# A Mamba block with quantised gate: softplus in phases, dt_proj's steps in a row, low-rank preparation by items, SiLU as one function

## Chip, cores and metric

One Trainium2 chip, one core. The time is device microseconds of one execution; all arrays are float32, the quantised weights int32.

## What is computed

x has the shape 2 x 1024 x 512 (batch, tokens, H). Cut to what matters:

```python
xn = layernorm(x)
p = xn @ in_proj_w                    # 512 -> x part 1024, z part 1024
xc = silu(conv4(x_part) + conv_b)     # causal, 4 taps, per channel
ssm = xc @ x_proj_w.T                 # 1024 -> 64: dt_r 32, B 16, C 16, each rmsnorm'd
dt = softplus(dt_r @ dt_proj_w.T + dt_bias)
h_t = exp(dt * A) * h_{t-1} + dt * B_t * xc_t     # 16 states a channel
y = (sum_n h * C + D * xc) * silu(z)
s = y @ out_proj_w.T
# qlinear: w = (q - 7.5) * scale * 0.005 ; x @ w.T + 0.02 * (x @ A @ B)
g = silu(qlinear_down(silu(qlinear_gate(xn)) * qlinear_up(xn)))
out = x + s * g
```

## The kernel before, in words

The program orders every engine's instructions by hand, with semaphores between them. It treats one batch b after the other, and within a batch two halves h of 512 channels (DH = 4 blocks of 128). TensorE is PE, VectorE DVE, ScalarE ACT, GpSimd POOL; SP issues most transfers, ACT's queue the stores of prepared weights.

**In_proj stage.** In eight rounds (m = 0 to 7) TensorE computes the x part of block m + 1 into one of two buffers of psA (`x_part`, L785, matmuls L748). ScalarE starts the convolution with bias and last tap (`start_conv`, L583), VectorE adds three taps (`conv`, L1032), ScalarE takes Tanh (L594), and VectorE makes silu from it (`conv_silu`, L1042; the taps were halved, L1022). TensorE's `x_proj(m-1)` (L790) follows x_part(m+1): per block eight matmuls with xc as the stationary operand and 64 columns to stream.

**Preparation, batch 0 only.** The FFN's weights become float weights with the low-rank product added. `ffn_weights(it)` (L992) on VectorE dequantises tile it (0 to 10: a gate and an up tile of 126 columns; 11 to 21: a tile of down) and adds the product that `low_rank(use)` (L752, matmuls L759 and L763, contraction over 32 rows) put into one of three PSUM banks. PT = 3 tiles go into each round, so the gate/up tiles are done in the first four rounds and down in the rest. Gate/up tiles go out to w_gu in device memory over ACT's queue (L602), with a wait for the additions, and come back in the scan stage. SP loads q tiles in a ring of three (`load_q`, L379).

**From x_proj to dt_proj.** ScalarE squares and copies the sums (L606, L607), VectorE reduces and scales them (L1057 to L1071), and TensorE turns them (L829); two quarters of the first `gate_up` (L766) stand before that. ScalarE copies the turned sums (L613).

**Softplus phase**, once per half. `dt_proj(i)` (L834) for the four channel blocks, and with it softplus as relu(v) + log(1 + exp(-|v|)) with a correction for what 1 + e loses in rounding: ScalarE makes |v| and relu (`relu_abs`, L617), exp and 1 + e (`one_plus_exp`, L628), Ln (`log`, L636). VectorE makes the correction (`lost`, L1074), takes it from the logarithm and adds relu (`softplus`, L1081: two steps). The blocks follow one another, with two temporaries for two blocks in turn. GpSimd multiplies dt by xc for blocks 0 to 2 (L522) and VectorE for block 3 (L1170). Beside this TensorE computes gate and up tiles (`ahead`), and in h=1 turns the sums of the half before back (`turn_back`, L848) for `finish_y` (L1090, two VectorE steps). A phase ends with four scans of state 0.

**Scan stage.** 16 states times four blocks a half: GpSimd makes dt·x·B (L529), ScalarE exp(dt·A) (L646), VectorE scans (L1104), TensorE transposes (L871). Beside it run gate/up, z and down. Then out_proj (L948) and the output.

Softplus after the phases' start, on ScalarE (L691 to L701):

```python
for i in range(DH):
    if i == 0 and h == 0: ahead(0)
    relu_abs(i)
    if i == 3: ahead(2 - h)
    if i: log(i - 1)
    one_plus_exp(i)
    if i == 1: ahead(1 - h)
```

## Time and profile before

| | |
|---|---|
| median of 3 runs | 1370.32 us (1368.41 to 1370.78) |
| the profiled execution's own time | 1369.48 us |
| its span, first to last instruction | 1367.7 us |
| mean granted TensorE clock | 0.938 |
| busy: PE, DVE, POOL, ACT | 88%, 75%, 56%, 54% of the span |

How to read it. Times are us from the start of the span. A timeline row gives start, length, engine, line, operation, output and inputs with their shapes, how many records are merged, and in brackets the idle time before and what ended it; the ends of matmuls are modelled and pass the next start by some 0.1 us, so a stretch is best taken from start to start. A float32 matmul leaves two records. A row by form gives the count, the busy time in all, the mean in ns of one, and the idle time before. A row of busy time by stretch gives the stretch and its length, then the busy us (and records) of PE, PEld (weight loads), DVE, ACT and POOL, the granted clock (1.00 is 2.4 GHz, 0.50 is 1.2), and the share and GB/s of the DMA engines.

### The profile page before, as it was taken

The page shows a single profiled execution, that of the slowest core. Times are in us where ns is not written, and L with a number is a line of the kernel's source. Part 1 is how long each engine was busy: PE and PEld are TensorE (multiplying, and loading weights), DVE is VectorE, ACT ScalarE, POOL GpSimd, SP SyncE. Part 2 cuts the span into 40 slices and gives each one's busy share as a digit, 9 for nine tenths or more (in the row PEclk, how much of TensorE's full clock was granted, in tenths as well). Part 3 has the DMA queues.
Part 4 walks back from the last instruction along what each step waited for, and adds up shares of the span by engine and source line. Part 5 has one row for each costly group of instructions (what it writes and reads, how often), then busy time and mean ns, then how long its engine had stood idle before and what let it go on. Part 6 is the DMA issues. An engine that isn't in the chain of part 4 may idle for free.

```text
span 1367.7 us, 13293 instructions
## 1 busy us (share of the span) xinstructions
PE 1208.3 (88%) x4598; PEld 662.3 (48%) x4598; DVE 1030.8 (75%) x827; ACT 735.3 (54%) x892; POOL 762.6 (56%) x418
## 2 busy tenths in 40 slices
PE   4999838999987799998999982999998779999898
PEld 3664415555543355555544541555554335555543
DVE  2866479999948999996415547999984899999631
ACT  3111577777728577773012266777762857777300
POOL 1000048999913799994130004899881379989411
PEclk9778879999999899999999977999999889999999
DMA  6542114999961199998701111499996119999841
GB/s 216 197 152 76 54 46 115 229 221 229 228 153 62 62 216 228 225 220 223 275 32 39 46 39 50 124 229 217 230 217 154 62 62 225 226 224 218 226 179 38
DMA packets 60612, 214.08 MB, mean 157 GB/s; under 512 B 6362, under 2 KB 6490, under 8 KB 60132
## 3 DMA queue, kind: packets, MB, share of 16 engines
q0 software_dynamic: 16128, 88.09, 33.5%
q1 hardware_dynamic: 42836, 119.50, 25.4%
q10 hardware_dynamic: 1584, 5.68, 1.0%
q8 instruction: 36, 0.59, 0.2%
q14 instruction: 28, 0.23, 0.1%
HBM read 102.18 MB, written 22.98 MB: 92 GB/s over the span
## 4 chain that ended last, share of the span: by engine, by line
PE 39%; POOL 32%; DVE 11%; issue 7%; DMA 6%; ACT 6%; POOLq 0%; SPq 0%; DVEq 0%; ACTq 0%
POOL ub L529 27%; PE psA L748 9%; PE psM L893 8%; PE psM L948 8%; POOL yT L540 4%; DVE hb L1104 4%; PE psT L871 4%; DMA yT<-yc 4%; PE psM L774 3%; PE psM L795 2%; DMA bn<-ss_rows_scratch 2%; DVE hb L973 1%; PE psT L759 1%; DVE ub L973 1%; DVE hb L1086 1%
## 5 line engine op out<-in xcount | busy, mean ns | idle before, releaser
L529 POOL TENSOR_TENSOR ub<-dtx,bn 128x1024 f32<-128x1024 f32 x256 | 646.3, 2580 | 72.8 <-DVE hb L1104 53.8
L1104 DVE TENSOR_TENSOR_SCAN hb<-psA,ub 128x1024 f32<-128x1024 f32 x256 | 579.8, 2281 | 24.4 <-POOL ub L529 13.3
L646 ACT ACTIVATE psA<-dt,cc 128x1024 f32<-128x1024 f32 x256 | 286.4, 1119 | 171.8 <-DVE hb L1104 171.1
L871 PE MATMUL psT<-ident,hb 128*128 128x128 f32 x2048 | 289.9, 280 | 92.3 <-DVE hb L1104 52.2
L774 PE MATMUL psM<-xnT,w_ts 128*126 128x512 f32 x704 | 343.9, 620 | 30.0 <-DVE hid L973 22.1
L871 PEld LDWEIGHTS psT<-ident,hb 128*128 128x128 f32 x2048 | 235.8, 142 | 261.7 <-issue 81.8
L665 ACT ACTIVATE yc<-psT,ssm 128x512 f32<-128x512 f32 x336 | 217.3, 678 | 45.9 <-PE psT L871 45.8
L522 POOL TENSOR_TENSOR dtx<-dt,xc 128x1024 f32<-128x1024 f32 x12 | 28.2, 2352 | 364.2 <-DVE dt L1088 364.2
L774 PEld LDWEIGHTS psM<-xnT,w_ts 128*126 128x126 f32 x704 | 128.0, 199 | 148.0 <-issue 122.4
L893 PE MATMUL psM<-w_dn,hid 126*128 126x512 f32 x352 | 170.3, 613 | 0.0
L973 DVE SCALAR_TENSOR_TENSOR yT<-psT,ssm,yT 128x512 f32<-128x512 f32 x144 | 105.4, 736 | 45.5 <-DMA yT<-yc 40.9
L748 PE MATMUL psA<-xnT,w_ts 128*128 128x512 f32 x256 | 125.9, 650 | 1.4 <-ACT xnT L574 1.4
L883 PE MATMUL psM<-xnT,w_ts 128*128 128x512 f32 x256 | 119.1, 593 | 0.0
L540 POOL DMA_DIRECT2D yT<-yc x112 | 110.0, 982 | 14.0 <-ACT yc L665 14.0
L948 PE MATMUL psM<-dt,xc 128*128 128x512 f32 x256 | 111.7, 592 | 0.0
L558 POOL TENSOR_TENSOR hid<-hid,dtx 128x512 f32<-128x512 f32 x16 | 20.1, 1263 | 130.3 <-DMA hid<-x_dram 76.8
L973 DVE SCALAR_TENSOR_TENSOR hb<-psA,cc,hb 128x1023 f32<-128x1023 f32 (+2 forms) x48 | 61.5, 1281 | 41.2 <-ACT hb L586 40.1
L893 PEld LDWEIGHTS psM<-w_dn,hid 126*128 126x128 f32 x352 | 63.9, 198 | 53.6 <-issue 53.6
L748 PEld LDWEIGHTS psA<-xnT,w_ts 128*128 128x128 f32 x256 | 52.6, 211 | 64.7 <-issue 62.6
L973 DVE SCALAR_TENSOR_TENSOR th<-th,psM 128x512 f32<-128x512 f32 (+1 forms) x92 | 61.4, 668 | 28.2 <-ACT th L687 17.6
L948 PEld LDWEIGHTS psM<-dt,xc 128*128 128x128 f32 x256 | 47.8, 190 | 56.0 <-issue 55.0
L687 ACT ACTIVATE th<-psM 128x512 f32<-128x512 f32 x48 | 28.1, 584 | 83.4 <-PE psM L893 76.4
(88 smaller groups left out, 785.8 us busy)
## 6 DMA issues: line engine op xcount, KB each, us to landing
yT<-yc POOLq DMA_DIRECT2D x112, 768.0 KB, 7.1
bn<-ss_rows_scratch SPq DMA_DIRECT2D x64, 512.0 KB, 6.1
w_ts<-w_gu_scratch SPq DMA_DIRECT2D x44, 504.0 KB, 4.5
w_ts<-w_in_dram SPq DMA_DIRECT2D x32, 256.0 KB, 4.4
z_scratch<-th SPq DMA_DIRECT2D x32, 256.0 KB, 4.5
hb<-z_scratch SPq DMA_DIRECT2D x16, 512.0 KB, 8.3
w_gu_scratch<-hid ACTq DMA_DIRECT2D x11, 504.0 KB, 3.1
yT<-x_dram SPq DMA_DIRECT2D x2, 2048.0 KB, 12.3
```

Of the source, the lines that this page charges most:

```text
L529: pool.tensor_tensor(ub[:, i % 2, :], dtx[:, i, :], bn[:, t, :], ALU.mult).then_inc(s_u, 1)
L540: pool.dma_start(yT[:, YD + e * YG:YD + e * YG + YG, :].rearrange("p a c -> p (a c)"), yc[:, ring(n, e), :, :].rearrange("p a c -> p (a c) ...
L646: act.activation(psA[:, i % 2, :], dt[:, i, :], ACT.Exp, scale=negA[:, h * DH + i, bass.ds(n, 1)]).then_inc(s_a, 1)
L665: act.activation(to, psT[:, Y_POS[tb] % 2, :], ACT.Copy, scale=ssm[:, tb, R + NS + n:R + NS + n + 1]).then_inc(s_tcp, 1)
L748: mm = pe.matmul(psA[:, dst, c * 512:(c + 1) * 512], w_is[:, t, k, :], xnT[:, k, c * 512:(c + 1) * 512], start=(k == 0), stop=(k == HK - 1))
L774: mm = pe.matmul(psM[0:IM, gu, :], w_ts[:, t, at:at + IM], xnT[:, k, h * CH:(h + 1) * CH], start=(k == 0), stop=(k == HK - 1))
L871: mm = pe.transpose(psT[:, at % 2, i * P:(i + 1) * P], hb[:, t * DH + i, tb * P:(tb + 1) * P], ident[:, :])
L883: mm = pe.matmul(psM[:, c, :], w_is[:, off % 2, k, :], xnT[:, k, c * 512:(c + 1) * 512], start=(k == 0), stop=(k == HK - 1))
L893: mm = pe.matmul(psM[:, j % 2, :], hid[0:IM, k, j * P:(j + 1) * P], w_dn[0:IM, k, :], start=(k == 0), stop=(k == IT - 1))
L948: mm = pe.matmul(psM[:, tb % 2, :], xc[:, k, tb * P:(tb + 1) * P], w_o[:, k, :], start=(k == 0), stop=(k == DB - 1))
L973: return dve.scalar_tensor_tensor(out=out, in0=in0, scalar=scalar, in1=in1, op0=op0, op1=op1)
L1104: dve.tensor_tensor_scan(hb[:, t * DH + i, :], psA[:, i % 2, :], ub[:, i % 2, :], 0.0, ALU.mult, ALU.add).then_inc(s_scan, 1)
```

## The change

- **Preparation by items.** `low_rank(j)` computes for item j the gate and the up product in turn, from one stacked pair of operands (gate in rows 0 to 31, up in 32 to 63, down in 64 to 95), and then down's. `dequantise(j)` and `add_low_rank(j)` do the same on VectorE. The eleven items lie evenly in the eight rounds (`prepared(m)`): two at m = 2, 5 and 7, otherwise one. Loads of q and stores of w_gu follow that order.
- **SiLU as one function.** ScalarE's Silu writes xc; the halving of the taps and VectorE's product go.
- **x_proj** has the weights as the stationary operand (64 columns) and streams xc, 512 columns a matmul, with the two halves of the tokens in the output partitions 0 to 63 and 64 to 127. The sums are then copied (xr) and turned by four transposes before the Square.
- **Softplus in phases.** ScalarE does four times Abs and Relu, then four times exp and 1 + e, then four Ln, then the decays. Temporaries are dtx[i] and ub or hb, one pair for each block. VectorE's `lost` also takes the correction from relu, in front of the logarithm, so that `softplus` is one step. dt·xc is VectorE's for all blocks (`drive`).
- **dt_proj** 0 to 3 stand in a row in h=0; in h=1 turn_back(0) and (1) stand before dt_proj(2) and (3). Gate/up comes behind them; only one quarter of it stays before the turning of the sums.

The diff, cut:

```diff
+def prepared(m):
+
+    return range(IT * m // DB, IT * (m + 1) // DB)
...
-            return (hb[:, DH, :], hb[:, DH + 3, :]) if i % 2 else (ub[:, 0, :], ub[:, 1, :])
+            return dtx[:, i, :], [ub[:, 0, :], ub[:, 1, :], hb[:, DH, :], hb[:, DH + 3, :]][i]
...
-                    for i in range(DH - 1):
-                        k = blk(b, h, i)
-                        pool.wait_ge(s_dt, k + 1)
-                        pool.tensor_tensor(dtx[:, i, :], dt[:, i, :], xc[:, h * DH + i, :],
-                                           ALU.mult).then_inc(s_dtxp, 1)
-                    pool.wait_ge(s_dtxp, (b * HALVES + h + 1) * (DH - 1))
...
                     act.wait_ge(s_af, a_use(b, m) + 3)
-                    act.activation(tmp[:, 2 + m % 2, :], tmp[:, m % 2, :], ACT.Tanh).then_inc(s_thc, 1)
-                    for j in range(PT):
-                        if m + 1 < DB and j == PT - 1:
-                            start_conv(m + 1)
-                        it = PT * m + j
-                        if b == 0 and it < IT:
-
-                            act.wait_ge(s_lrr, 2 * it + 5)
-                            act.dma_start(w_gu[it], wf[:, it % QD, :]).then_inc(s_wst[it % QD], 16)
-
-                v = psM[:, 0, :].rearrange("p (a e) -> p a e", e=E)
+                    act.activation(xc[:, m, :], tmp[:, m % 2, :], ACT.Silu).then_inc(s_xc, 1)
+                    if m + 1 < DB:
+                        start_conv(m + 1)
+                    if b == 0:
+                        for j in prepared(m):
+
+                            act.wait_ge(s_lrr, 3 * j + 5)
+                            act.dma_start(w_gu[j], wf[:, j % QD, :]).then_inc(s_wst[j % QD], 16)
+
                 act.wait_ge(s_xp, b + 1)
+                act.activation(xr, psM[:, 0, :], ACT.Copy).then_inc(s_xr, 1)
+                v = psT[:, 0, :].rearrange("p (a c e) -> p c a e", c=2, e=E)
+                act.wait_ge(s_xt, b + 1)
                 act.activation(sq, v, ACT.Square).then_inc(s_sq, 1)
-                act.activation(ssm[:, :, :], v, ACT.Copy).then_inc(s_xpr, 1)
+                act.activation(ssm[:, :, :].rearrange("p (c a) e -> p c a e", c=2), v, ACT.Copy).then_inc(s_xpr, 1)
...
-                        if i >= 2:
-                            act.wait_ge(s_dt, k - 1)
+                        if b and h == 0 and i == 0:
+                            act.wait_ge(s_o, b * TB)
...
                     for i in range(DH):
-                        if i == 0 and h == 0:
+                        relu_abs(i)
+                    if h == 0:
+                        ahead(0)
+                    for i in range(DH):
+                        one_plus_exp(i)
+                        if h == 0 and i == 2:
+                            ahead(1)
+                        if h and i == 1:
                             ahead(0)
-                        relu_abs(i)
-                        if i == 3:
-                            ahead(2 - h)
-                        if i:
-                            log(i - 1)
-                        one_plus_exp(i)
-                        if i == 1:
-                            ahead(1 - h)
+                    for i in range(DH):
+                        log(i)
+                    if h:
+                        ahead(1)
 
                     act.wait_ge(s_dtr, blk(b, h, DH))
                     for i in range(DH):
                         act.wait_ge(s_dt, blk(b, h, i) + 1)
                         decay(0, i)
-                        if i == 0:
-                            log(DH - 1)
-                        if i == 1 and h:
+                        if i == 1:
                             ahead(2)
...
+            def low_rank(j):
+
+                pe.wait_ge(s_lrr, 3 * j + 3)
+                at = slice(j * IM, (j + 1) * IM)
+                for k in range(HK):
+                    for gu in range(2):
+                        rows = slice(gu * R, (gu + 1) * R)
+                        mm = pe.matmul(lr_bank(gu)[:, k * IM:(k + 1) * IM], la[rows, k * P:(k + 1) * P],
+                                       lb[rows, at], start=True, stop=True)
+                        if k == HK - 1:
+                            mm.then_inc(s_lr, 1)
+                rows = slice(2 * R, 3 * R)
+                pe.matmul(lr_bank(2)[0:IM, :], la[rows, at], lb[rows, 0:H], start=True, stop=True).then_inc(s_lr, 1)
...
-                    for tb in range(TB):
-                        mm = pe.matmul(psM[:, 0, tb * E:(tb + 1) * E], xc[:, k, tb * P:(tb + 1) * P], wx[:, k, :],
-                                       start=(k == 0 and tb == 0), stop=(k == DB - 1 and tb == TB - 1))
+                    for c in range(2):
+                        mm = pe.matmul(psM[c * E:(c + 1) * E, 0, :], wx[:, k, :], xc[:, k, c * CH:(c + 1) * CH],
+                                       start=(k == 0), stop=(k == DB - 1))
...
                 for m in range(DB):
                     if m + 1 < DB:
                         x_part(m + 1)
                     if b == 0:
 
-                        for use in range(lr_uses(m) + 3, min(lr_uses(m + 1) + 3, LR_USES)):
-                            low_rank(use)
+                        for j in prepared(m):
+                            if j + 1 < IT:
+                                low_rank(j + 1)
                     if m > 0:
                         x_proj(m - 1)
                 x_proj(DB - 1).then_inc(s_xp, 1)
                 if b == 0:
                     pe.wait_ge(s_lrr, LR_USES + 3)
 
-                pe.wait_ge(s_xpr, b + 1)
-                for q in range(2):
-                    gate_up(b, 0, 0, 0, q, landed(b, w_half(0, 0)))
+                pe.wait_ge(s_xr, b + 1)
+                for a in range(JD):
+                    mm = pe.transpose(psT[:, 0, a * P:(a + 1) * P], xr[:, a * P:(a + 1) * P], ident[:, :])
+                mm.then_inc(s_xt, 1)
+                gate_up(b, 0, 0, 0, 0, landed(b, w_half(0, 0)))
...
                     dt_proj(0)
                     dt_proj(1)
-                    if h:
-                        turn_back(0)
-                    else:
-
-                        for q in range(2, 4):
-                            gate_up(b, 0, 0, 0, q, landed(b, w_half(0, 0)))
-                    dt_proj(2)
-                    if h:
-                        turn_back(1)
-                    ahead(1 - h)
-                    dt_proj(3)
+                    for i in range(2):
+                        if h:
+                            turn_back(i)
+                        dt_proj(2 + i)
                     if h:
                         turn_back(2)
-                    ahead(2 - h)
-                    if h:
                         turn_back(3)
-                    for n in range(3 - h, FILL):
+                        ahead(0)
+                    else:
+                        for q in range(1, 4):
+                            gate_up(b, 0, 0, 0, q, landed(b, w_half(0, 0)))
+                    for n in range(1, FILL):
...
+            def dequantise(j):
+
+                t, turn = j % QD, 2 * j
+                dve.wait_ge(s_q[turn % QD], 16 * (turn // QD) + 16)
+                dve.wait_ge(s_wst[t], 16 * (j // QD) + 16)
+                for gu in range(2):
+                    sl = slice(gu * HK * IM, (gu + 1) * HK * IM)
+                    at = (2 * j + gu) * IM
+                    scale = scales[:, at:at + IM].rearrange("p (k i) -> p k i", k=1).to_broadcast([P, HK, IM])
+                    ins = stt(wf[:, t, sl].rearrange("p (k i) -> p k i", k=HK),
+                              qs[turn % QD][:, sl].rearrange("p (k i) -> p k i", k=HK), -Q_ZERO, scale, ALU.add, ALU.mult)
+                ins.then_inc(s_deq, 1)
+                turn += 1
+                dve.wait_ge(s_q[turn % QD], 16 * (turn // QD) + 16)
+                stt(w_dn[0:IM, j, :], qs[turn % QD][0:IM, 0:H], -Q_ZERO, scales[0:IM, 2 * IT * IM:], ALU.add,
+                    ALU.mult).then_inc(s_deq, 1)
+
+            def add_low_rank(j):
+
+                dve.wait_ge(s_deq, 2 * j + 2 + QD)
+                for gu in range(2):
+                    w = wf[:, j % QD, gu * HK * IM:(gu + 1) * HK * IM]
+                    dve.wait_ge(s_lr, 3 * j + gu + 1)
+                    stt(w, lr_bank(gu)[:, 0:HK * IM], LR_SCALE, w, ALU.mult, ALU.add).then_inc(s_lrr, 1)
+                w = w_dn[0:IM, j, :]
+                dve.wait_ge(s_lr, 3 * j + 3)
+                stt(w, lr_bank(2)[0:IM, :], LR_SCALE, w, ALU.mult, ALU.add).then_inc(s_lrr, 1)
...
+                        dequantise(prepared(m)[0])
                     if b == 0:
-                        for it in range(PT * m + 1, min(PT * (m + 1), 2 * IT)):
-                            ffn_weights(it)
+                        for j in prepared(m):
+                            if j > prepared(m)[0]:
+                                dequantise(j)
+                            add_low_rank(j)
...
                         stt(e, w, -1.0, e, ALU.add, ALU.subtract).then_inc(s_nd, 1)
+                        dve.wait_ge(s_nd, k + 1)
+                        dve.wait_ge(s_dtr, k + 1)
+                        dve.tensor_tensor(dt[:, i, :], dt[:, i, :], e, ALU.subtract).then_inc(s_rl, 1)
 
                     def softplus(i):
                         k = blk(b, h, i)
                         e, w = soft_tmp(i)
-                        dve.wait_ge(s_nd, k + 1)
+                        dve.wait_ge(s_rl, k + 1)
                         dve.wait_ge(s_ln, k + 1)
-                        dve.tensor_tensor(e, w, e, ALU.subtract).then_inc(s_rl, 1)
-                        dve.wait_ge(s_rl, k + 1)
-                        dve.tensor_tensor(dt[:, i, :], dt[:, i, :], e, ALU.add).then_inc(s_dt, 1)
+                        dve.tensor_tensor(dt[:, i, :], dt[:, i, :], w, ALU.add).then_inc(s_dt, 1)
...
+                    def drive(i):
+
+                        softplus(i)
+                        dve.wait_ge(s_dt, blk(b, h, i) + 1)
+                        dve.tensor_tensor(dtx[:, i, :], dt[:, i, :], xc[:, h * DH + i, :], ALU.mult).then_inc(s_dtx, 1)
+
+                    if h:
+                        for i in range(DH):
                             finish_y(i)
-                        if i == 1:
-                            silu_gate(1 - h, 1 - h)
-                        softplus(i)
-                        if i == 1:
-                            hidden(1 - h, 1 - h)
-
-                    dve.wait_ge(s_dt, blk(b, h, DH))
-                    dve.tensor_tensor(dtx[:, DH - 1, :], dt[:, DH - 1, :], xc[:, h * DH + DH - 1, :],
-                                      ALU.mult).then_inc(s_dtx, 1)
+                    else:
+                        silu_gate(0, 0)
+                    lost(0)
+                    if h == 0:
+                        dve.wait_ge(s_out, b * (TB * 16) + 16)
+                        hidden(0, 0)
+                    lost(1)
+                    if h:
+                        silu_gate(0, 0)
+                    lost(2)
+                    if h:
+                        hidden(0, 0)
+                    else:
+                        silu_gate(1, 1)
+                    lost(3)
+                    drive(0)
+                    if h:
+                        silu_gate(1, 1)
+                    drive(1)
+                    hidden(1, 1)
+                    drive(2)
                     scan(0, 0, 0)
-                    if h:
-                        hidden(1, 1)
+                    drive(3)
                     scan(0, 0, 1)
-                    if h:
-                        silu_gate(2, 0)
+                    silu_gate(2, 0)
                     scan(0, 0, 2)
                     scan(0, 0, 3)
```

## Rows read from the trace of the kernel before

**Rows 1.** The page, the chain that ended last: share of the span by engine.
```profile
PE 39%; POOL 32%; DVE 11%; issue 7%; DMA 6%; ACT 6%; POOLq 0%; SPq 0%; DVEq 0%; ACTq 0%
```

**Rows 2.** Busy time by stretch of two rounds, batch 0; x_proj's weight loads by form.
```profile
68.00:86.70 18.70, 18.70 (x81) 13.16 (x82) 13.07 (x19) 2.26 (x2) 0.00 (x0) 0.77 0.46 166
...
103.10:116.10 13.00, 13.00 (x41) 6.48 (x40) 9.05 (x11) 2.26 (x2) 0.00 (x0) 0.89 0.28 80
...
L795 PEld LDWEIGHTS psM<-hb,xc 128*128 128x128 f32 x256 | 36.7, 227 | 13.5 <-DVE xc L973 7.3 <-issue 6.1
```

**Rows 3.** Timeline of PE in the preparation: start, length, engine, line, what, records.
```profile
31.91 1.95 PE L759 MATMUL psT<-dtx,hid 32*128 32x126 f32 x16
...
103.13 8.24 PE L748 MATMUL psA<-xnT,w_ts 128*128 128x512 f32 x16
111.31 1.12 PE L763 MATMUL psT<-dtx,hid 32*126 32x512 f32 x2
...
114.07 2.23 PE L795 MATMUL psM<-hb,xc 128*128 128x64 f32 x16
...
129.21 8.78 PE L748 MATMUL psA<-xnT,w_ts 128*128 128x512 f32 x16
...
145.70 3.06 PE L795 MATMUL psM<-hb,xc 128*128 128x64 f32 x16 [2.94 <-DVE xc L973]
```

**Rows 4.** Timelines of DVE and ACT in batch 0's last round; additions by form.
```profile
139.27 3.92 DVE L973 SCALAR_TENSOR_TENSOR hb<-psA,cc,hb 128x1023 f32<-128x1023 f32 x3 [4.29 <-ACT hb L586]
...
148.79 0.60 ACT L606 ACTIVATE hb<-psM 128x512 f32<-128x512 f32 x1 [4.51 <-PE psM L795]
...
L973 DVE SCALAR_TENSOR_TENSOR hid<-psT,hid 128x504 f32<-128x504 f32 x14 | 9.2, 677 | 0.2
```

**Rows 5.** Timelines of PE and ACT in in_proj of batch 1.
```profile
773.86 1.90 PE L795 MATMUL psM<-hb,xc 128*128 128x64 f32 x16
775.59 7.09 PE L748 MATMUL psA<-xnT,w_ts 128*128 128x512 f32 x16
...
787.91 1.06 ACT L594 ACTIVATE hb<-hb 128x1024 f32<-128x1024 f32 x1 [3.98 <-DVE hb L973]
```

**Rows 6.** Timelines of DVE and PE between the squares and dt_proj, batch 0.
```profile
152.74 0.69 DVE L1069 TENSOR_TENSOR ssm<-ssm,lnw 128x512 f32<-128x512 f32 x1
...
149.97 5.29 PE L774 MATMUL psM<-xnT,w_ts 128*126 128x512 f32 x8 [1.22 <-issue]
155.10 1.04 PE L829 MATMUL psT<-ident,ssm 128*64 128x128 f32 x8
156.86 4.06 PE L844 MATMUL psA<-hb 32*128 32x512 f32 x8 [0.72 <-ACT hb L613]
```

**Rows 7.** Busy time by stretch: two of 1 us in dt_proj, batch 0, h=0.
```profile
159.00:160.00 1.00, 1.00 (x4) 0.37 (x2) 0.44 (x1) 1.00 (x2) 0.00 (x0) 1.00 0.22 49
160.00:161.00 1.00, 1.00 (x3) 0.15 (x1) 0.00 (x0) 1.00 (x2) 0.00 (x0) 0.53 0.00 0
```

**Rows 8.** ACT: first Abs of h=0, and the loads in front of Ln.
```profile
158.88 1.11 ACT L625 ACTIVATE ub<-psA,cc 128x1024 f32<-128x1024 f32 x1 [0.16 <-PE psA L844]
...
L641 ACT ACT_TABLE_LOAD x16 | 20.5, 1283 | 7.9 <-DVE hb L973 6.9 <-DVE ub L973 0.9
```

**Rows 9.** Timelines of DVE and POOL in softplus of h=0, batch 0.
```profile
163.06 1.22 DVE L973 SCALAR_TENSOR_TENSOR ub<-ub 128x1024 f32<-128x1024 f32 x1 [3.62 <-ACT ub L634]
...
179.88 2.62 DVE L973 SCALAR_TENSOR_TENSOR ub<-ub 128x1024 f32<-128x1024 f32 x1 [0.30 <-ACT ub L634]
...
179.05 2.37 POOL L522 TENSOR_TENSOR dtx<-dt,xc 128x1024 f32<-128x1024 f32 x1 [6.63 <-DVE dt L1088]
```

**Rows 10.** Third and fourth scan of h=0; scans of h=1; PE of h=1.
```profile
203.85 4.59 DVE L1104 TENSOR_TENSOR_SCAN hb<-psA,ub 128x1024 f32<-128x1024 f32 x2 [0.34 <-POOL ub L529]
...
455.57 4.46 DVE L1104 TENSOR_TENSOR_SCAN hb<-psA,ub 128x1024 f32<-128x1024 f32 x2
...
404.00 3.69 PE L844 MATMUL psA<-hb 32*128 32x512 f32 x8
```

124 lines of the change are left out of this document (32 added, 92 removed).

## The prediction

> **What bounds the kernel now.** I read first the chain that ended last [rows 1]: no engine holds it alone, TensorE has 39% and GpSimd 32%. GpSimd's share is the product of the scan loop, which the change does not touch, so I looked for the stages that are touched. They are four kinds: the preparation beside in_proj in batch 0 (about 24 to 149 us), in_proj of batch 1 (718 to 794), the short chain from the squares to the first dt_proj of each batch, and four softplus phases, from the first Abs to the fourth scan.
>
> In the preparation TensorE is busy without a gap, and the granted clock is what varies [rows 2]: a round with nine low-rank products takes 18.7 us at 0.77, one with three 13.0 us at 0.89. The rows of the second kind [rows 3] show how a round is built: x_part 8.2 us, low rank 2.8 (111.3 to 114.07), x_proj 2.0. TensorE is the bound in each round up to 138.0. Then a tail follows, in which the last convolution, Tanh and product run alone and x_proj(7) after them: from the end of x_part(7) at 138.0 to the Square at 148.8 are 10.8 us [rows 3, 4]. In batch 1 the period is 8.65 us, x_part 6.92 and x_proj 1.73 [rows 5], so TensorE bounds it too.
>
> A softplus phase is a ping-pong of ScalarE and VectorE: 49.6 us in h=0 from the first Abs at 158.88 to the end of the fourth scan at 208.44 [rows 8, 10], and 52.5 in h=1 (first Abs at 407.5, when the second dt_proj is done, end at 460.0) [rows 10]. What I looked for there is what VectorE would do if ScalarE were not in its way, since the change takes loads of tables off ScalarE.
>
> **Part 1, the preparation (batch 0).** The eleven gate/up pairs and the eleven down tiles go through in eleven items of two dequantised gate/up tiles and one of down, one or two items a round (two at m = 2, 5 and 7), where before the heavy items came first. An item is 16 small matmul records and 2 large. Nearest rows: 16 small ones take 1.9 us [rows 3], and three down products 2.8 us, so 0.95 for one: 2.8 for an item, as long as a round's low rank at 111 us. A round with one item therefore stays at 13.0, one with two lies between 13.0 + 2.8 + 0.7 (it waits until VectorE has emptied all three banks) = 16.5 and the 18.7 of rows 2. I take 18.7, since that round holds a similar run of small matmuls. From the start of x_part(1) at 33.8: 11.0 (no x_proj yet) + 3 x 13.0 + 2 x 18.7 + 8.8 = 96.2, so x_part(7) ends at 130.0 instead of 138.0: 8.0 us less (12.4 at 16.5 a round).
>
> The tail gives it back. low_rank(10) stands in TensorE's order in front of x_proj(6) and x_proj(7), and waits for the additions of item 9, which VectorE does behind convolution 7. From the end T of x_part(7): convolution done at T+5.2 [rows 4], three dequantising steps and three additions of 0.65 each [rows 4] at T+9.1. Then item 10 (2.8 at full clock, 5.3 at half), x_proj(6) and (7) in the new form (8 records of 512 columns, 0.43 each at full clock [rows 5], so 3.5 or 6.9), the copy of the sums 0.7 and the new transposes (1.0 [rows 6], or 1.9). Square starts at T+17.2 at full clock, T+24 at half, against T+10.8 now. TensorE stands idle before, and x_proj(7) after such a wait takes 3.06 us for what takes 1.73 in the stream [rows 3, 5], so I take T+21.3: 10.5 more. Part 1: +2.5, between -6 (16.5 a round, full clock) and +6 (18.7, half clock).
>
> The removed product of silu on VectorE (1.22 us) and the removed halving are covered: VectorE idles in every round. Silu takes Tanh's place on ScalarE; no row has it, and I take Tanh's 1.06 us [rows 5]; half or twice of that moves only the two tails, by 0.5 or 1.1, as the step is covered in all other rounds. On ScalarE's queue the next start_conv now stands in front of the stores of w_gu and their waits, behind which it stood before; in the one-item rounds it was TensorE that ended last anyway, so nothing for it. The queue of SP carries the same tiles in another order, behind the same w_in loads; the two low-rank loads are longer, and are needed only at 30.9 when x_part(0) is done.
>
> **Part 2, in_proj of batch 1.** x_proj becomes 4 records of 512 columns on 64 stationary columns: 4 x 0.43 = 1.73, what it takes now [rows 5]. Nothing for it in the rounds; if one record of four runs beside another, -0.4 a round (-3), if changing between shapes costs a tenth of a microsecond each way, +1.5. At the end of the stage 1.25 us of VectorE go, copy and transposes come with 1.7 to 2.6: +1. Part 2: +1, between -3 and +3.
>
> **Part 3, squares to first Abs, twice.** Only half as much of gate/up stands before the transposes of the sums. They are ready at 153.4 and run at 155.10 behind gate/up [rows 6]: 1.6 less if the clock is full. But TensorE does less just before; at half clock the transposes cost 0.9 and dt_proj(0) 1.9 more. I take -0.5 each, -1 together, between -3.2 and +5.6.
>
> **Part 4, softplus, four phases.** Off ScalarE go most loads of 1.28 us (four Ln loads a phase [rows 8] become one, and as many returns to Exp). What becomes late next is VectorE. In h=0: four Abs/Relu pairs 8.4, a load and a Tanh 1.9, first Exp and 1+e 2.1 puts the first correction at 12.4 after the first Abs. From there VectorE is never free: four corrections of 2.45 (two steps of 1.22) 9.8, four pieces of gate and hidden 2.6, four times softplus and dt·x 9.8, four scans 9.1 [rows 9, 10]. GpSimd's products for the scan run between. The rows show what that does: a VectorE step of 1.22 us takes 2.62 when GpSimd started at 179.05, it ends 1.1 us after GpSimd does [rows 9]. Three products of 2.35 each stand in the way, less 0.65 that reads PSUM beside one: 6.4. Sum 12.4 + 9.8 + 2.6 + 9.8 + 9.1 + 6.4 = 50.1, against 49.6. So the removed loads buy nothing here: +0.5 with a full clock. The dt·x that moved from GpSimd to VectorE costs 3 x 1.22 of this.
>
> The Trainium skill, in SBUF — State Buffer (the two separate sides), says that such a pair of ports is an exclusive lock for a whole instruction. By that rule the trace agrees.
>
> The clock speaks against the four dt_proj in a row. Two of them are done at full clock, and right behind them the granted clock is 0.53 [rows 7]; gate/up then runs between now and brings it back. With four in a row the third and fourth, 2.0 us each [rows 6], take up to 3.5: from 0 to +3.0, I take +2. So h=0 costs 2.5 each, +5 for two. In h=1 four finish_y (each about 2.5, behind the turn_backs) put the first correction at 13.7: 13.7 + 9.8 + 3.2 + 9.8 + 9.1 + 5.7 = 51.3 against 52.5. With 1.2 lost to the clock: 0 each. Part 4: +5. At full clock it is 2 x 0.5 - 2 x 1.2 = -1.4, and -6 if GpSimd's products cost a fifth less; at half clock for both dt_proj 2 x 3.5 + 2 x 2 = +11. The first Abs of batch 1 now also waits for the last add_x of batch 0, which lies a whole in_proj stage earlier: nothing.
>
> Sum: +2.5 + 1 - 1 + 5 = +7.5 on the profiled execution's 1369.48 gives 1377. That execution is 0.8 us under the median 1370.32.
>
> **The rivals.** A: *small matmuls of different rows run beside each other.* The change writes gate and up with rows 0 to 31 and 32 to 63 in turn. Against: x_proj now shows 0.108 us for a load of 128 columns with only 64 columns to stream, so the load is the price [rows 2, 5], and 16 loads stay. For: none of the rows has two row groups in use, so none can exclude it. If it halves them, 0.9 an item (-10 for eleven), the clock is kept in the two long rounds (-4), x_proj loses 0.4 x 16 (-6): 7.5 - 20 = -12.5, 1357. The Trainium skill, TensorEngine Tiling (Array Packing), Key Properties, says that different tiles can load and multiply in parallel; no run here shows it yet. Chance 0.30.
>
> B: *the clock stays full* in dt_proj and the tail, since the new records have more columns each: part 1 -6, part 2 +1, part 3 -3, part 4 -1.4: -9, 1360. Against: the fall in rows 7. Chance 0.12.
>
> C: *TensorE at half clock through the tail, dt_proj and the first gate/up after it*. Then Tanh waits for gate/up too, and all later steps with it: the upper ends of all parts, 6 + 3 + 5 + 11 = +25, 1394. It decides if dt_proj(0) already starts at half. Chance 0.12.
>
> **How the numbers follow.** My case has 0.46, and its own range is 1366 to 1387. What a measurement of this kernel tells from no change is 0.2%, 2.7 us. Faster: nearly all of A, most of B, a little of mine: 0.41. Same: 0.13. Slower: 0.46. The range must reach into A and nearly to C: 1353 to 1390.
>
> **What would show it.** In the profile after, x_part(7) ends near 130, low_rank(10) starts 9 us later with x_proj(6) behind it, and Square is near 151. The 16 small records of an item take 1.9 us (mine) or 1.0 (A). In a phase VectorE is busy from the first correction to the fourth scan, softplus steps of 1.2 appear as 2.5 beside GpSimd, and the phase lasts 50 to 53 us. Wrong I am if the phases fall under 48, or if Square is before 142.

## The result, and the profile after

The changed kernel takes 1346.59 us (median of four, 1339.98 to 1352.72) against 1369.37 of the kernel before in the same session: ratio 0.9847, 95% interval 0.9814 to 0.9880. Measured once more beside later runs it has 0.9874 (0.9854 to 0.9895), so the two bracket 0.986. It is faster by 1.3 to 1.5%, where I had forecast 1377 and a range from 1353: the direction of rival A, and more of it than A gave. Its runs scatter more than those of before; in the two profiled executions the first Square lies at 124.7 and at 128.2 us. The profiled execution shown here took 1344.27, with a span of 1342.5 against 1367.7.

| milestone, us (profiled executions) | before | forecast | after |
|---|---|---|---|
| end of x_part(7), batch 0 | 138.0 | 130.0 | 107.1 |
| from there to the Square | 10.8 | 21.3 | 17.6 |
| Square of batch 0 | 148.8 | 151.3 | 124.7 |
| Square to first Abs, batch 0, 1 | 10.1, 10.0 | 9.6, 9.5 | 9.1, 11.3 |
| period of a block in in_proj of batch 1 | 8.65 | 8.65 | 8.07 |
| first Abs to fourth scan, h=0 of batch 0, 1 | 49.6, 51.2 | 52.1 | 52.3, 52.5 |
| the same, h=1 of batch 0, 1 | 52.5, 52.6 | 52.5 | 55.7, 50.9 |

The chain that ended last can't be set beside [rows 1]: it comes out cut off, with a quarter of the span in it. So I read stages. The timeline of TensorE in the changed kernel's preparation answers [rows 3]: start, length, engine, line, what, records.

```profile
31.15 0.37 PE L753 MATMUL psM<-dtx,hid 32*128 32x126 f32 x1
31.16 0.37 PE L753 MATMUL psT<-dtx,hid 32*128 32x126 f32 x1
31.36 0.27 PE L753 MATMUL psM<-dtx,hid 32*128 32x126 f32 x1
31.37 0.27 PE L753 MATMUL psT<-dtx,hid 32*128 32x126 f32 x1
...
31.71 0.69 PE L758 MATMUL psT<-dtx,hid 32*126 32x512 f32 x1
...
32.24 0.59 PE L758 MATMUL psT<-dtx,hid 32*126 32x512 f32 x1
32.76 7.13 PE L742 MATMUL psA<-xnT,w_ts 128*128 128x512 f32 x16
...
50.66 1.08 PE L789 MATMUL psM<-xc,hb 128*64 128x512 f32 x4
...
107.10 0.37 PE L753 MATMUL psM<-dtx,hid 32*128 32x126 f32 x1
...
116.11 0.58 PE L753 MATMUL psM<-dtx,hid 32*128 32x126 f32 x1 [6.32 <-DVE w_dn L964]
...
119.14 3.68 PE L789 MATMUL psM<-xc,hb 128*64 128x512 f32 x8
```

Gate's and up's records start 0.01 us apart, in pairs, and the down record at 31.71 starts in the middle of them: three row groups are at work at once. An item takes from 31.15 to 32.76, 1.6 us, where I had 2.8; x_proj takes 1.0 where I had 1.73; and x_part itself takes 7.13 us, the length at full clock, in six of its seven rounds (8.42 in the other), where before it took 8.2 to 9.7. The busy time by stretch shows it as the clock (columns: stretch, length, busy PE, PEld, DVE, ACT, POOL, granted clock, share of the DMA engines, GB/s). Of before, the same four stretches:

```profile
24.00:52.00 28.00, 28.00 (x108) 16.68 (x109) 19.32 (x23) 5.80 (x5) 0.00 (x0) 0.86 0.41 136
52.00:78.00 26.00, 26.00 (x106) 16.41 (x105) 16.70 (x23) 2.26 (x2) 0.00 (x0) 0.83 0.55 189
78.00:110.00 32.00, 32.00 (x117) 19.87 (x116) 23.02 (x29) 4.52 (x4) 0.00 (x0) 0.79 0.40 134
110.00:125.00 15.00, 15.00 (x43) 7.18 (x42) 8.85 (x10) 2.54 (x3) 0.00 (x0) 0.89 0.25 78
```

and after:

```profile
24.00:52.00 28.00, 27.43 (x107) 12.28 (x108) 18.44 (x21) 7.04 (x7) 0.00 (x0) 1.00 0.38 125
52.00:78.00 26.00, 24.49 (x95) 10.31 (x94) 18.75 (x25) 4.52 (x4) 0.00 (x0) 0.87 0.53 170
78.00:110.00 32.00, 30.29 (x132) 13.06 (x130) 25.84 (x34) 6.78 (x6) 0.00 (x0) 1.00 0.54 180
110.00:125.00 15.00, 7.79 (x30) 3.27 (x30) 9.64 (x14) 1.93 (x3) 0.00 (x0) 0.62 0.33 118
```

TensorE was busy without a gap before, at 0.79 to 0.89; after it has a gap now and then and is at full speed through most of it. The last stretch is the tail: TensorE waits 6.3 us for item 9 and then works at half clock.

The softplus of h=0, batch 0: VectorE after, against [rows 9, 10], with GpSimd's product of the scan.

```profile
147.94 0.69 DVE L964 SCALAR_TENSOR_TENSOR th<-th,psM 126x512 f32<-126x512 f32 x1 [18.58 <-ACT th L644]
149.97 1.23 DVE L964 SCALAR_TENSOR_TENSOR dtx<-ub,dtx 128x1024 f32<-128x1024 f32 x1 [1.34 <-ACT ub L627]
...
163.15 1.22 DVE L1076 TENSOR_TENSOR dt<-dt,ub 128x1024 f32<-128x1024 f32 x1
164.41 3.25 DVE L1144 TENSOR_TENSOR dtx<-dt,xc 128x1024 f32<-128x1024 f32 x1
...
172.34 2.28 DVE L1092 TENSOR_TENSOR_SCAN hb<-psA,ub 128x1024 f32<-128x1024 f32 x1
...
175.77 3.25 DVE L1144 TENSOR_TENSOR dtx<-dt,xc 128x1024 f32<-128x1024 f32 x1
```

```profile
163.38 3.19 POOL L522 TENSOR_TENSOR ub<-dtx,bn 128x1024 f32<-128x1024 f32 x1 [141.54 <-issue]
...
174.76 3.17 POOL L522 TENSOR_TENSOR ub<-dtx,bn 128x1024 f32<-128x1024 f32 x1 [4.68 <-DVE hb L1092]
```

The first correction stands at 149.97, 16 us behind the first Abs (133.84), and from there VectorE has no gap until the scans. Beside GpSimd's product its 1.22 us become 3.0 to 3.25, and GpSimd's own 2.35 become 3.2 where VectorE was first. The rows add up to taking turns: VectorE's step of 163.15 ends at 164.37, GpSimd's product ends 2.2 us later (166.57), and VectorE's next step ends 1.1 us after that (167.66).

### The profile page after: what moved, and what is told of

Read it like the earlier page. It is cut to its first block and busy times, and to the rows that moved or that the text cites. A ratio compares the mean times of both kernels' runs of the same rounds, so it can differ in the third digit from the quotient of the medians.

```text
span 1342.5 us, 12891 instructions
## 1 busy us (share of the span) xinstructions
PE 1186.8 (88%) x4414; PEld 623.9 (46%) x4414; DVE 1016.6 (76%) x822; ACT 705.0 (53%) x870; POOL 733.7 (55%) x406
## 5 line engine op out<-in xcount | busy, mean ns | idle before, releaser
L1092 DVE TENSOR_TENSOR_SCAN hb<-psA,ub 128x1024 f32<-128x1024 f32 x256 | 579.7, 2281 | 22.9 <-POOL ub L522 10.2
L867 PE MATMUL psT<-ident,hb 128*128 128x128 f32 x2048 | 289.6, 280 | 89.1 <-DVE hb L1092 52.3
L768 PE MATMUL psM<-xnT,w_ts 128*126 128x512 f32 x704 | 348.3, 628 | 19.8 <-DVE hid L964 12.1
L867 PEld LDWEIGHTS psT<-ident,hb 128*128 128x128 f32 x2048 | 238.9, 143 | 256.6 <-issue 86.7
L658 ACT ACTIVATE yc<-psT,ssm 128x512 f32<-128x512 f32 x336 | 217.4, 678 | 49.5 <-PE psT L867 49.4
L889 PE MATMUL psM<-w_dn,hid 126*128 126x512 f32 x352 | 167.6, 605 | 0.0
L742 PE MATMUL psA<-xnT,w_ts 128*128 128x512 f32 x256 | 114.9, 603 | 1.4 <-ACT xnT L566 1.4
L889 PEld LDWEIGHTS psM<-w_dn,hid 126*128 126x128 f32 x352 | 62.9, 195 | 52.2 <-issue 52.2
L742 PEld LDWEIGHTS psA<-xnT,w_ts 128*128 128x128 f32 x256 | 48.0, 192 | 67.3 <-issue 65.5
L964 DVE SCALAR_TENSOR_TENSOR dtx<-psM,dtx 128x512 f32<-128x512 f32 x16 | 11.0, 690 | 80.5 <-PE psM L939 80.5
## 6 DMA issues: line engine op xcount, KB each, us to landing
yT<-x_dram SPq DMA_DIRECT2D x2, 2048.0 KB, 12.5
```

The source lines that it names most:

```text
L658: act.activation(to, psT[:, Y_POS[tb] % 2, :], ACT.Copy, scale=ssm[:, tb, R + NS + n:R + NS + n + 1]).then_inc(s_tcp, 1)
L742: mm = pe.matmul(psA[:, dst, c * 512:(c + 1) * 512], w_is[:, t, k, :], xnT[:, k, c * 512:(c + 1) * 512], start=(k == 0), stop=(k == HK - 1))
L768: mm = pe.matmul(psM[0:IM, gu, :], w_ts[:, t, at:at + IM], xnT[:, k, h * CH:(h + 1) * CH], start=(k == 0), stop=(k == HK - 1))
L867: mm = pe.transpose(psT[:, at % 2, i * P:(i + 1) * P], hb[:, t * DH + i, tb * P:(tb + 1) * P], ident[:, :])
L889: mm = pe.matmul(psM[:, j % 2, :], hid[0:IM, k, j * P:(j + 1) * P], w_dn[0:IM, k, :], start=(k == 0), stop=(k == IT - 1))
L964: return dve.scalar_tensor_tensor(out=out, in0=in0, scalar=scalar, in1=in1, op0=op0, op1=op1)
```

## The experiments

**Where the preparation's gain comes from.** Two runs take one part out of the changed kernel, a third puts one part alone into the kernel before.

```diff
-        la = hid_flat[0:3 * R, QD * WT:QD * WT + IT * IM]
-        lb = dtx_flat[0:3 * R, 0:IT * IM]
+        la = hid_flat[0:R, QD * WT:QD * WT + 2 * H + IT * IM]
+        lb = dtx_flat[0:R, 0:2 * IT * IM + H]
...
-                        rows = slice(gu * R, (gu + 1) * R)
-                        mm = pe.matmul(lr_bank(gu)[:, k * IM:(k + 1) * IM], la[rows, k * P:(k + 1) * P],
-                                       lb[rows, at], start=True, stop=True)
+                        at = gu * H + k * P
+                        to = (gu * IT + j) * IM
+                        mm = pe.matmul(lr_bank(gu)[:, k * IM:(k + 1) * IM], la[:, at:at + P],
+                                       lb[:, to:to + IM], start=True, stop=True)
```

> The changed kernel, with the low-rank factors of gate, up and down all in rows 0 to 31 of the array, as before the change; order and shape of the matmuls stay. Row tiles run beside each other (theory): an item, 1.6 us in the changed kernel, grows to about 2.8 us as the prediction had it when every weight load takes its turn; 11 items, so the first Square of batch 0 moves from 124.7 to 134 to 140 us, and the ratio to the kernel before rises from 0.985 to 0.992 to 0.996. The rows have no part in it and the even spreading of the items made the gain (rival): the item stays within 0.2 us of 1.6, the Square at 124.7, the ratio at 0.985.

On the host the factors are laid side by side for this (left out here). Ratio 0.9988 (0.9974 to 1.0003): almost the whole gain of the change is gone. TensorE's timeline of this run, the same item:

```profile
31.43 0.48 PE L753 MATMUL psM<-dtx,hid 32*128 32x126 f32 x2
31.75 0.38 PE L753 MATMUL psT<-dtx,hid 32*128 32x126 f32 x2
...
33.31 1.02 PE L758 MATMUL psT<-dtx,hid 32*126 32x512 f32 x2
34.26 0.70 PE L742 MATMUL psA<-xnT,w_ts 128*128 128x512 f32 x1
```

Now the records go one after the other, 0.22 us for a pair, and an item takes 31.43 to 34.26, 2.8 us: my figure, for a kernel in which the rows are shared. Of the 16 to 19 us, 11 x 1.2 = 13 are the items, and some 3 more are clock and wait in the rounds with two items: such a round takes 17.7 and 18.2 us here (x_part starts at 55.07, 72.77 and 96.60, 114.81) and 14.9 and 12.9 in the changed kernel (14.3 and 15.2 in its repeat). The Square is at 142.9, later than the 134 to 140 expected.

The clock is not the rows' doing. Busy time by stretch in this run, the first three of the four stretches above:

```profile
24.00:52.00 28.00, 27.64 (x91) 13.80 (x91) 16.87 (x19) 6.78 (x7) 0.00 (x0) 1.00 0.35 107
52.00:78.00 26.00, 25.05 (x82) 12.54 (x81) 18.56 (x24) 3.86 (x4) 0.00 (x0) 0.80 0.51 170
78.00:110.00 32.00, 31.05 (x116) 16.43 (x114) 21.12 (x26) 5.72 (x5) 0.00 (x0) 0.96 0.45 153
```

With the rows shared, the granted clock from 24 to 125 us is 0.90, against 0.83 before and 0.91 in the changed kernel; x_part takes 7.13 in five of seven rounds, and a round with one item and x_proj takes 10.9 us (85.69 to 96.60), not 13.0. The next run, with the old x_proj, has 0.90 too. So with either of the two taken out the clock stays up. Whether each of them suffices, or the even spreading of the items does it, no run separates.

```diff
-                    for c in range(2):
-                        mm = pe.matmul(psM[c * E:(c + 1) * E, 0, :], wx[:, k, :], xc[:, k, c * CH:(c + 1) * CH],
+                    for tb in range(TB):
+                        mm = pe.matmul(psM[:, 0, tb * E:(tb + 1) * E], xc[:, k, tb * P:(tb + 1) * P], wx[:, k, :],
```

> The changed kernel with the x_proj of before (eight column blocks of the activations as stationary operand, no copy and no transposes behind it). Column halves run beside each other (theory): a block's x_proj grows from 1.0 to 1.9 us; seven of them stand in rounds that TensorE bounds in each batch, so 6 us more in either batch, less the copy and the transposes behind them (about 1.9 us each time): 8 us more, ratio 0.991. Column halves don't matter or are hidden (rival): only the copy and the transposes are seen, 3 to 4 us less, ratio 0.982.

The copy and the transposes behind it go as well. Ratio 0.9892 (0.9854 to 0.9931), near the theory's 0.991, but its interval overlaps those of both measurements of the changed kernel, so the total alone doesn't show a difference. The stages do: the period of a block in batch 1 is back at 8.65, and the Square of batch 0 is at 135.3 us. (The profiled execution is the slowest of its four, 1364.5 against a median of 1354.0, so not all of those 10.6 us are the columns'.) TensorE's timeline of batch 0 shows the old step at both clocks:

```profile
65.95 3.67 PE L787 MATMUL psM<-hb,xc 128*128 128x64 f32 x16
...
117.76 2.00 PE L787 MATMUL psM<-hb,xc 128*128 128x64 f32 x16
```

From its start to the next x_part's it takes 3.5 at half clock (65.95 to 69.42) and 1.8 at full (50.90 to 52.73), against 1.0 for the four records at 50.66 in the changed kernel, where x_part follows at 51.67. The new form has four records of 512 columns, and 512 columns take 0.43 us in turn; so the column halves run beside each other as the row groups do. Not all of it arrives: in batch 1 a block has 8.07 us where x_part alone (6.92) and two pairs of 0.43 make 7.78. The 0.29 between lies at the two changes of shape; the first step of x_part takes 0.54 there instead of 0.43.

> The kernel before with one edit, Silu as one function in place of Tanh and the combining step on VectorE. TensorE bounds the rounds (theory): the step on VectorE was no part of the bound, the period of the blocks in batch 1 stays at 8.7 us and the ratio at 0.998 to 1.000. The wait for the combining step set the pace (rival): 1.2 us less for each of 8 blocks in batch 1 and 5 to 10 us in batch 0, ratio 0.988 to 0.992.

Edit: `ACT.Silu` for `ACT.Tanh`, the combining step and the halving of the taps left out. Ratio 0.9955 (0.9936 to 0.9974), between the two: the period in batch 1 stays at 8.65, as the theory has it, but in_proj ends 2.2 us earlier in batch 0 (Square at 146.6), and in batch 1 it takes 1.3 us less to the Square. That the last block has no cover fits this; it was not tested apart. The rest of the 6 us I don't find: the profiled execution is the slowest of the five (1366.6, median 1360.2) and shows only 2.9 us less of span than before.

**The tail of the preparation.** Two runs move items away from it; both stand on the run with the old softplus (e3, below) and are read against that.

```diff
-    return range(IT * m // DB, IT * (m + 1) // DB)
+    at = (0, 2, 3, 5, 6, 8, 9, 10, 11)     # e8: (0, 2, 3, 5, 6, 8, 9, 11, 11)
+    return range(at[m], at[m + 1])
```

> The kernel of the run with the old softplus, with the 11 items as 2, 1, 2, 1, 2, 1, 1, 1 over the eight rounds, one in the last round and not two. The end of the preparation is a chain behind the last item on VectorE (theory: TensorE idle for 6.3 us ahead of it): one item's 4 us on VectorE leave the end, the earlier rounds take 3 us more for it only once; Square 3 to 5 us earlier, ratio 0.973 against 0.976. The round that gets the item grows by as much (rival): 0.976.

> The same with 2, 1, 2, 1, 2, 1, 2, 0: no item in the last round. Theory: nothing stands between the last convolution and x_proj any more, TensorE isn't idle ahead of it and keeps its clock; Square 8 to 11 us earlier than at 125.5, less 3 us for the second item in the round before; ratio 0.971. Rival: VectorE's work is only moved, 0.976.

Ratios 0.9793 (0.9758 to 0.9828) and 0.9777 (0.9747 to 0.9807) against 0.9764: both theories fall. The Square stays at 127.8 and 127.5, against 125.5. With no item in the last round TensorE's groups of the preparation show where the wait went:

```profile
L762 PE MATMUL psM<-dtx,hid 32*128 32x126 f32 x88 | 14.0, 302 | 5.5 <-DVE w_dn L979 5.5
L798 PE MATMUL psM<-xc,hb 128*64 128x512 f32 x32 | 11.1, 791 | 4.5 <-ACT xc L596 4.5
```

10.0 us of waits in place of 9.8 that stood in front of the low-rank products alone: the last x_proj now waits for the last convolution and Silu, and an earlier round for its second item.

**The softplus.** First the whole of it undone, then its parts.

> The changed kernel with the softplus of before on all engines (two blocks in turn, dt_proj steps with gate/up between them, products dt*x of blocks 0 to 2 on GpSimd). The phases are a loss (theory, from the stretch first Abs to fourth scan, 52.3, 55.7 and 52.5 us after against 49.6, 52.5 and 51.2 before): 2 to 3 us less in each of four, 7 to 9 us in all, ratio 0.979. The phases are part of the gain, through fewer table loads (rival): the ratio rises to 0.988 or more. Neither: 0.985.

Edit: before's order of dt_proj, of the functions, of VectorE's steps and before's products on GpSimd, in the changed kernel. Ratio 0.9764 (0.9740 to 0.9787), 1334.45 us: the phases are a loss of about 1%, and the rest of the change is worth 2.4%. The four stretches from first Abs to fourth scan are 51.3, 52.5, 49.6 and 52.2 us, 205.6 together, which is what they were before (205.9), against 211.4 in the changed kernel. Of the 9.8 us between the two spans this is 5.8. Of the other 4.0, 2.1 lie between Square and first Abs of batch 1 (9.2 here, 11.3 in the changed kernel) and about 4 in the loops between the stretches; 2.2 come back ahead of the first Abs of batch 0. For the 2.1 the rows show the clock. TensorE's dt_proj there, in this run (two of them) and in the changed kernel (four):

```profile
774.92 3.69 PE L849 MATMUL psA<-hb 32*128 32x512 f32 x8 [0.73 <-ACT hb L615]
```

```profile
778.88 14.02 PE L840 MATMUL psA<-hb 32*128 32x512 f32 x16 [0.68 <-ACT hb L606]
```

Here two quarters of gate/up stand in front of the transposes, which take 1.04 us, and dt_proj starts at full clock. In the changed kernel one quarter stands there, the transposes take 1.89, and dt_proj is at half clock from its start.

> The changed kernel, phases kept, with the products dt*x of blocks 0 to 2 on GpSimd again. VectorE's own work is what makes the phases longer (theory): three instructions of 1.22 us leave it in each of four softplus stretches, 2 to 3 us less in each, ratio 0.978. What GpSimd's products take back from VectorE while they run is as much (rival; before the change 1.4 us beside each of three): ratio 0.984 to 0.987.

```diff
+                    for i in range(DH - 1):
+                        pool.wait_ge(s_dt, blk(b, h, i) + 1)
+                        pool.tensor_tensor(dtx[:, i, :], dt[:, i, :], xc[:, h * DH + i, :],
+                                           ALU.mult).then_inc(s_dtxp, 1)
```

Ratio 0.9911 (0.9882 to 0.9939): if anything slower than the changed kernel, which neither expectation had. GpSimd's and VectorE's timelines:

```profile
161.53 8.78 POOL L528 TENSOR_TENSOR dtx<-dt,xc 128x1024 f32<-128x1024 f32 x3 [139.55 <-DVE dt L1083]
170.38 4.64 POOL L523 TENSOR_TENSOR ub<-dtx,bn 128x1024 f32<-128x1024 f32 x2
```

```profile
172.82 2.29 DVE L1099 TENSOR_TENSOR_SCAN hb<-psA,ub 128x1024 f32<-128x1024 f32 x1 [7.02 <-POOL ub L523]
```

Three products in a row on GpSimd take 8.8 us, and the first product of the scan comes behind them: VectorE waits 7.0 us. In the phases the blocks become ready close together, so what was spread between the blocks before now stands in a queue.

> The changed kernel with the three remaining gate/up steps of item 0 put between dt_proj of blocks 1 and 2 in the first half of each batch, so that the four dt_proj's are not in a row. The falling clock of the four in a row costs (theory: 3.4 us from one first function on ScalarE to the next where two of ScalarE's own take 2.1): the clock stays higher, though the third block comes 2.6 to 5 us later, and the tanh of item 0 is there at once; ratio 0.982. ScalarE and VectorE have work enough (rival): 1 to 3 us more in each of two stretches, ratio 0.987.

```diff
                    dt_proj(1)
+                    if h == 0:
+                        for q in range(1, 4):
+                            gate_up(b, 0, 0, 0, q, landed(b, w_half(0, 0)))
                     for i in range(2):
```

The three quarters of gate/up leave their place behind the fourth dt_proj. Ratio 0.9924 (0.9895 to 0.9952): the other way. The clock does come back, and it doesn't pay. TensorE in h=0, first this run, then the changed kernel:

```profile
131.77 4.97 PE L840 MATMUL psA<-hb 32*128 32x512 f32 x8 [0.68 <-ACT hb L606]
136.67 7.49 PE L768 MATMUL psM<-xnT,w_ts 128*126 128x512 f32 x12
144.09 3.70 PE L840 MATMUL psA<-hb 32*128 32x512 f32 x8
```

```profile
131.75 11.82 PE L840 MATMUL psA<-hb 32*128 32x512 f32 x16 [0.68 <-ACT hb L606]
```

Two dt_proj take 3.7 us after gate/up, near the 4.06 for two of [rows 6], and 5 to 7 in a row; but the third starts at 144.1 instead of 136.5, and the stretch grows from 52.3 to 56.5. So the clock isn't worth a later third block. What the phases lack might be an early start for VectorE, which the next run tests. The changed kernel ran again beside it:

> The changed kernel as it is, beside the next run: its four times so far lie from 1340 to 1353 us, wider than those of the run with the old softplus (1332 to 1336). Ratio 0.985 within 0.003.

Ratio 0.9874 (0.9854 to 0.9895).

```diff
                     for i in range(DH):
                         relu_abs(i)
-                    if h == 0:
-                        ahead(0)
-                    for i in range(DH):
                         one_plus_exp(i)
-                        if h == 0 and i == 2:
-                            ahead(1)
-                        if h and i == 1:
-                            ahead(0)
+                        if h == 0 and i == 2:
+                            ahead(0)
+                    if h:
+                        ahead(0)
                     for i in range(DH):
                         log(i)
-                    if h:
-                        ahead(1)
+                    ahead(1)
```

VectorE's corrections, finish_y and gate steps follow in that order.

> The changed kernel with the softplus of one block's Abs, Relu, Exp and 1+e in a row, block after block, and only the four logarithms as a phase behind them (VectorE's correction of a block goes between; its number of instructions stays, and so do the table loads, within one). What the phases cost is VectorE's idle time at their start (theory: 14 us from the first Abs to its first correction in the trace of the changed kernel, then 25 us without a gap): the first correction comes 4 to 5 us behind the first Abs, ScalarE's 4.3 us a block also covers a dt_proj of 3.4 us at half clock; first Abs to fourth scan falls from 52.3 to 44 us in a first half and from 55.7 to 48 in a second; 25 to 30 us in four stretches, ratio 0.964 to 0.968. VectorE's total and GpSimd's hold on it set the length (rival): 2 us or less in each, ratio 0.980 to 0.985.

Ratio 0.9767 (0.9729 to 0.9804). VectorE's timeline, the first corrections:

```profile
139.81 1.23 DVE L960 SCALAR_TENSOR_TENSOR dtx<-ub,dtx 128x1024 f32<-128x1024 f32 x1 [10.23 <-ACT ub L627]
141.07 1.23 DVE L1065 TENSOR_TENSOR dt<-dt,dtx 128x1024 f32<-128x1024 f32 x1
143.85 1.23 DVE L960 SCALAR_TENSOR_TENSOR dtx<-ub,dtx 128x1024 f32<-128x1024 f32 x1 [1.55 <-ACT ub L627]
```

The first correction comes 5.6 us behind the first Abs (134.21) instead of 16. The stretches are 48.0, 49.5, 48.9 and 48.3, 194.7 together: 16.7 less than in the changed kernel, and its span is 16.2 shorter. I had expected 44 and 48. The number of table loads is the changed kernel's, 17 (41 before), and one of 1.28 us still stands in front of the first Exp; GpSimd's hold is still there too. The next two runs take the hold away, once with the phases and once blockwise.

```diff
-                        pool.wait_ge(s_dtx, blk(b, h, i) + 1)
+                        pool.wait_ge(s_dtx, blk(b, h, DH - 1) + 1)
                         input(0, 0, i)
...
-                    scan(0, 0, 0)
                     drive(3)
+                    scan(0, 0, 0)
```

> The changed kernel, phases kept; only GpSimd's first product dt*x*B waits until all four products dt*x are there, and VectorE does the fourth ahead of the first scan. GpSimd's hold on VectorE is a part of the phases' price (theory: in the changed kernel three of VectorE's 1.22 us instructions take 3.0 to 3.25 us beside GpSimd's product, and GpSimd's 2.35 us products take 3.2): these 6 us leave, and 2.4 us in which VectorE waits for the first product come in their place; 3 us less in each of four stretches, ratio 0.978 against 0.986. GpSimd's later start costs what the hold did (rival): 0.985 to 0.988.

> The blockwise softplus of the run before with the same hold on GpSimd's first products and the fourth dt*x ahead of the first scan. Theory: first Abs to fourth scan, 48 to 49.5 us there, falls by 3 to 5 us in each of four; ratio 0.965. Rival: as with the phases, the late start takes the gain; ratio 0.975 to 0.978.

Ratios 0.9777 (0.9749 to 0.9805) and 0.9650 (0.9635 to 0.9665), both as the theory had them. The stretches follow it only in part. With the phases they are 49.3, 53.5, 49.7 and 54.0: 3 us less in each h=0, as expected, but in h=1 no less than in the repeat of the changed kernel (53.4 and 53.9). Blockwise the hold takes 3.6, 1.3, 3.7 and 1.8 us off them, where 3 to 5 were expected in each. Where the rest of the two gains lies I have not found. VectorE and then GpSimd in the second:

```profile
168.84 1.22 DVE L1140 TENSOR_TENSOR dtx<-dt,xc 128x1024 f32<-128x1024 f32 x1
169.98 0.68 DVE L960 SCALAR_TENSOR_TENSOR hid<-th,psM 126x512 f32<-126x512 f32 x1
172.65 4.60 DVE L1088 TENSOR_TENSOR_SCAN hb<-psA,ub 128x1024 f32<-128x1024 f32 x2 [1.99 <-POOL ub L522]
```

```profile
170.20 4.65 POOL L522 TENSOR_TENSOR ub<-dtx,bn 128x1024 f32<-128x1024 f32 x2 [148.30 <-issue]
```

All eight TENSOR_TENSOR steps of this part are back at 1.22, GpSimd's product at 2.33; the price is one wait of 2.0 us. The scans run beside GpSimd at their own 2.28 in the kernels shown. The stretches are 44.4, 48.2, 45.2 and 46.6 us, 184.4 together. At 1319.13 us (1317.38 to 1324.03) this version beats both kernels: 3.5% under before, 2.0 to 2.3% under the changed one. It computes all that they compute; only the orders shown differ from the changed kernel.

## Why the prediction was wrong

**Part 1, the step that failed: "2.8 for an item".** It took all records in turn, 16 small ones in 1.9 us and one down tile in 0.95. Measured: 1.6 for the item, with gate, up and down on three row groups side by side; the same item on shared rows takes the 2.8. It is this step that put x_part(7) at 130.0: it ends at 107.1, and on shared rows at 123.4, so 16.3 of the 22.9 us are the rows'. The mechanism was on record as rival A with 0.30, and its price of 0.9 an item was too low, since I halved only the small records and left the down tile beside nothing. The rule named there (the Trainium skill, TensorEngine Tiling (Array Packing), Key Properties: different tiles can load and multiply in parallel) is what the trace shows, for rows in fp32 and for column halves too. The argument against it, that x_proj's load sets its pace, was right about the price of the old x_proj and said nothing about whether two loads exclude each other. Nor is the load the only price: 126 columns at the pace of the 512-column records (0.43) are 0.106 us, the same as the load, so for the small records these traces can't tell the two apart; the 512-column records of x_proj are longer than their load and run side by side all the same.

**The second failed term: "13.0 a round".** It held x_part at 8.2 us, so at the clock of before. At full clock it is 7.13, and a round with one item 9.7 = 7.13 + 1.6 + 1.0. I moved work in a stretch whose clock was 0.79 to 0.89 and kept the clock. This term was wrong for the kernel that I had in mind too: on shared rows the round takes 10.9, and the Square comes at 142.9 where I had 151.3. Why the clock stays up is open. The two rounds of two items I took at 18.7; they are 14.9 and 12.9, and 17.7 and 18.2 with shared rows, so for those the bound from [rows 2] was a fair one.

**The tail held in kind.** low_rank(10) starts 9.0 us after x_part(7), forecast 9.1, at half clock as forecast; behind it everything is shorter by the side-by-side tiles (item 3.0 for 5.3, x_proj twice 3.7 for 6.9). 17.6 instead of 21.3. (The upper end of part 1 was summed wrongly: 24 - 10.8 - 8.0 is +5.2, not +6.)

**Part 2.** +1 forecast, measured -4.6 (75.5 us from the start of in_proj of batch 1 to its Square before, 70.8 after). With the old x_proj it is 74.2, so 3.4 of it are the column halves, 0.6 a block (A had 0.4); the other 1.3 the kernel before gains from Silu alone (74.2 too). The bound for changes of shape, a tenth of a microsecond each way, was about right: 0.29 for two. **Part 3.** -1 forecast, measured +0.3 by the table: the transposes and the first dt_proj of batch 1 are at half clock, within the bounds.

**Part 4: the sum held, in part by luck.** +5 forecast, +5.5 measured over the four stretches (211.4 against 205.9); h=0 was forecast at 52.1 and is 52.3 and 52.5. Inside it the first correction comes 16.1 us behind the first Abs and not 12.4, because the four pairs of Abs and Relu follow dt_proj at half clock, 3.4 us apart (11.9 for the 8.4); I had +2 for that. The rest takes 36.2 and not 37.7. In h=1, where I had nothing, it is +3.2 and -1.7. And 49.6 was my base for both h=0, where batch 1 had 51.2: there the level was right, the difference (+1.3 for +2.5) not. The rule cited for the lock (the Trainium skill, SBUF — State Buffer, the two separate sides) fits: the rows above add up to taking turns, and e11 shows the hold with the order that goes with it to be worth 0.7 to 1.0%. But e3 puts the whole price of the phases at about 1%, twice the part that the stretches show; of the rest only the 2.1 us ahead of the first Abs of batch 1 are placed, at half clock.

**The rivals.** A's mechanism is shown; its total is not its -12.5 but -18 to -23 by the two measurements, and the clock that it counted as the rows' is kept in more rounds, and without the rows too. B fell: the clock is 0.5 to 0.6 in dt_proj and the tail. C's condition was met in batch 1 (dt_proj at 0.50 throughout) and cost 2.1 us ahead of the first Abs, not 25: the Tanh that it had waiting for gate/up waits 0.3 and 0.15 us in the two batches. My two marks for being wrong, a Square before 142 and a phase under 48, split: the first was met (124.7), the second wasn't.

Added up against the first measurement of the changed kernel, rows 1.4%, columns 0.45 (not clear of noise), Silu 0.45 and softplus -0.8 make 1.5%, which is the gain; against the second they make 1.1 + 0.2 + 0.45 - 1.1 = 0.7 of 1.3. So between nothing and 0.6% is left for the even spreading of the items, which was not run alone.

## What to carry to other kernels

Where fp32 matmuls fill only a part of the array (32 rows, or 64 stationary columns), put them on row or column groups of their own and issue them in turn: here the row groups, an item in 1.6 us for 2.8, were worth 1.1 to 1.4%, as much as the whole change gained on balance. TensorE's clock rose in the same stage, but it rose without them as well; take it as a term of its own. Judge phases by when the next engine can start, not by the table loads that they save: twelve fewer loads per batch gained nothing while VectorE stood idle for 16 us, and Abs to 1+e block by block with only Ln as a phase kept the few loads and started VectorE 5.6 us behind the first Abs. Hold GpSimd's elementwise products back until VectorE is in instructions that they don't slow, such as the scans here.
